# A recurrent block with top-2 experts: logits of all sequences in front, experts' blocks from the ninth FFN tile on

## The reference

```python
xn = layernorm(x)
# branch 1: gated linear recurrence, then a gated FFN
h = rmsnorm(xn) * pre_norm_w
a, i, v = sigmoid(h @ w_a + bias), sigmoid(h @ w_i), h @ w_v
s = sqrt(clip(1 - a*a, 1e-8)) * (i * v)
rec[t] = a[t] * rec[t-1] + s[t]              # scanned in chunks of 64
x1 = xn + rec @ out_proj_w
g, u = split(rmsnorm(x1) * ffn_norm_w @ w_gate_up)   # 2 x 1024 columns
y1 = x1 + (silu(g) * u) @ w_down
# branch 2: top 2 of 8 experts per token
w_tok = softmax over the two largest of xn @ w_router
y2 = sum_e w_tok[e] * (relu(xn @ w_fc[e])**2 @ w_proj[e])
out = x + y1 + y2
```

## Time and profile before

| | us |
|---|---|
| median of 3 runs | 336.8 (336.75 to 338.13) |
| profiled execution | 335.52 |
| its span | 333.8 |
| TensorE busy | 295.5 |
| VectorE busy | 200.8 |
| ScalarE busy | 171.5 |
| POOL busy | 156.3 |

### The profile page before, as it was taken

The page is one execution under the profiler, slowest core; times in us unless marked ns, Lnnn a source line. Parts: engine busy times, 40 slices in busy tenths (PEclk is TensorE's granted clock), DMA queues, the critical chain, the costliest instruction groups (busy, mean ns, idle before and its releaser), DMA issues.

```text
span 333.8 us, 5643 instructions
## 1 busy us (share of the span) xinstructions
PE 295.5 (89%) x1842; PEld 260.8 (78%) x1842; DVE 200.8 (60%) x460; ACT 171.5 (51%) x361; POOL 156.3 (47%) x130
## 2 busy tenths in 40 slices
PE   6589979957685889799899998999999989999993
PEld 6568868746574778698799997889999778888882
DVE  2277747889998984368845555884565552343332
ACT  2669737726836333664336557443655752222220
POOL 5523121500860335748765866786586664316000
PEclk9779979979969899979999999999999999999999
DMA  6999910007030102433433444334443452919931
GB/s 218 355 385 372 422 62 0 0 2 196 0 111 17 34 16 51 65 50 51 66 64 65 65 66 66 64 63 67 67 64 66 64 62 34 165 26 156 226 124 64
DMA packets 31228, 34.29 MB, mean 103 GB/s; under 512 B 5088, under 2 KB 28896, under 8 KB 31168
## 3 DMA queue, kind: packets, MB, share of 16 engines
q0 software_dynamic: 11712, 14.58, 27.7%
q1 hardware_dynamic: 16560, 17.25, 15.2%
q10 hardware_dynamic: 2928, 2.10, 2.0%
HBM read 22.06 MB, written 13.96 MB: 108 GB/s over the span
## 4 chain that ended last, share of the span: by engine, by line
PE 72%; DVE 15%; ACT 4%; issue 3%; DMA 2%; POOL 2%; SPq 1%; DVEq 0%; ACTq 0%; POOLq 0%
PE ps L353 60%; PE ps L411 5%; PE ps L545 4%; DMA X<-in_L_attn_x_dram 2%; PE ps L379 2%; ACT h L704 1%; DVE at_lane L1018 1%; PE ps L424 1%; DVE hT_lo L887 1%; DVE gu L1064 1%; PE ps L362 1%; DVE one_of L1028 1%; DVE dec L921 1%; DVE nblk L984 1%; DVE h2T_lo L936 1%
## 5 line engine op out<-in xcount | busy, mean ns | idle before, releaser
L1281 POOL DMA_INDIRECT xg<-xh_dram,gather_u x39 | 49.5, 1270 | 55.4 <-DVE picks L1094 30.5
L1290 POOL DMA_INDIRECT acc_dram<-yb,gather_u x39 | 62.4, 1599 | 15.2 <-issue 8.6
L353 PE MATMUL ps<-h2T_lo,Wgu_hi 128*128 128x512 f32 x128 | 43.4, 400 | 0.0
L353 PE MATMUL ps<-Wd_hi,guT_hi 128*128 128x256 f32 x128 | 37.2, 291 | 6.8 <-DVE guT_lo L1069 6.8
L353 PE MATMUL ps<-h2T_hi,Wgu_hi 128*128 128x512 f32 x128 | 40.8, 400 | 0.7 <-DVE h2T_lo L936 0.7
L1064 DVE TENSOR_TENSOR gu<-gu,ps 128x512 f32<-128x512 f32 x32 | 21.9, 685 | 30.9 <-PE ps L353 30.8
L353 PE MATMUL ps<-h2T_hi,Wgu_lo 128*128 128x512 f32 x128 | 40.2, 396 | 0.0
L353 PE MATMUL ps<-Wd_hi,guT_lo 128*128 128x256 f32 x128 | 37.0, 289 | 0.0
L353 PE MATMUL ps<-Wd_lo,guT_hi 128*128 128x256 f32 x128 | 37.0, 289 | 0.0
L724 ACT ACTIVATE gu<-ps 128x512 f32<-128x512 f32 x32 | 19.1, 597 | 34.1 <-PE ps L353 34.0
L1111 DVE TENSOR_TENSOR aT_lo<-ps,aT_hi 128x256 fp32r<-128x256 f32 x39 | 16.5, 424 | 27.4 <-ACT aT_hi L754 25.1
(11 more groups left out here) (167 smaller groups left out, 691.6 us busy)
## 6 DMA issues: line engine op xcount, KB each, us to landing
X<-acc_dram POOLq DMA_DIRECT2D x8, 512.0 KB, 9.1
acc_dram<-zero SPq DMA_DIRECT2D x1, 2176.0 KB, 14.3
X<-in_L_attn_x_dram SPq DMA_DIRECT2D x4, 512.0 KB, 8.0
Wgu_raw<-in_L_attn_w_gate_up_dram SPq DMA_DIRECT2D x4, 512.0 KB, 9.8
xh_dram<-X ACTq DMA_DIRECT2D x4, 512.0 KB, 7.5
Wfc_raw<-in_L_ffn_w_fc_dram SPq DMA_DIRECT2D x4, 512.0 KB, 11.5
Wpj_raw<-in_L_ffn_w_proj_dram SPq DMA_DIRECT2D x4, 512.0 KB, 4.0
out_dram<-X SPq DMA_DIRECT2D x3, 512.0 KB, 6.1
```

The costliest lines, as they stand in the source:

```text
L353: return nc.tensor.matmul(dst, lhs, rhs, start=start, stop=stop, skip_group_check=group)
L1281: pool.indirect_dma_start(out=xg[i % XG][:, :], out_offset=None, in_=xh_dram, in_offset=bass.IndirectOffsetOnAxis(ap=gather_u[:, i:i + 1], ...
L1290: pool.indirect_dma_start(out=acc_dram[i % 2], in_=yb[i % YB][:, :], in_offset=None, compute_op=ALU.add, out_offset=bass.IndirectOffsetOnA ...
```

## The change

`FIRST` goes from 4 to 8 and `LAST` from 19 to 24: there are eight bare tiles ahead of the blocks and seven behind them, and 17 tiles with the 39 blocks. Sequence 1's recurrence is run by VectorE among the bare tiles 2 to 4, its output projection by TensorE behind `down(3)` in tile 4, and the transposes of its second norm in tile 6, both in PSUM banks 6 and 7 (`aside`). The projections of sequences 2 and 3 stand behind tiles 11 and 17, the transposes behind 13 and 20, and their recurrences in 9, 10 and 15, 16.

In the front, TensorE has each sequence's transposes and logits earlier among the projections, so that all logits are done before sequence 0's output projection. ScalarE splits a sequence as soon as it is transposed; sequences 2 and 3 are normalised by VectorE instead of ScalarE. VectorE has `take_logits` and `top_two` ahead of sequence 1's gated values, and `take_counts` ahead of sequence 0's residual. The halves of the transposed input get a place each (sequence 3 shares that of 0). The experts' weights are split one by one between the bare tiles. POOL computes the second norm's root for sequence 1 ahead of the first gather.

```diff
+        hT = [(put(f"hT{c}_hi", [P, K, S], F32R, at), put(f"hT{c}_lo", [P, K, S], F32R, at + 4 * KB))
+              for c, at in enumerate((Wpj_hi_at, h2T_at[0], Wpj_hi_at + 8 * KB, Wpj_hi_at))]
         gain = [put(f"gain{b}", [P, K, S], F32, at)
-                for b, at in enumerate((cum_at, Wpj_hi_at, Wpj_hi_at + 4 * KB, cum_at))]
+                for b, at in enumerate((cum_at, cum_at, Wpj_hi_at + 8 * KB, Wpj_hi_at + 12 * KB))]
-        FIRST = 4
-        LAST = 19
-
-        PROJECT = {5: 1, 9: 2, 15: 3}
-        TURN = {6: 1, 12: 2, 18: 3}
+        FIRST = 8
+        LAST = 24
+
+        PROJECT = {11: 2, 17: 3}
+        TURN = {13: 2, 20: 3}
+
+        SLOTS, PROJECT_1, TURN_1 = 3, 4, 6
...
@@ TensorE's queue
-            for n in range(4):
-                aiv(0, n)
+            aiv(0, 0)
+            aiv(0, 1)
             transpose_x(1)
+            aiv(0, 2)
+            aiv(0, 3)
+            logits(0)
             aiv(0, 4)
             aiv(0, 5)
-            logits(0)
+            transpose_x(2)
             aiv(1, 0)
+            logits(1)
             aiv(1, 1)
-            transpose_x(2)
-            for n in range(2, 4):
-                aiv(1, n)
-            logits(1)
-            for n in range(4, 6):
-                aiv(1, n)
             transpose_x(3)
             logits(2)
+            aiv(1, 2)
+            logits(3)
+            aiv(1, 3)
             output_projection(0, 0)
             output_projection(0, 1)
-            logits(3)
-            for n in range(4):
+            aiv(1, 4)
+            aiv(1, 5)
+            count()
+            for n in range(6):
                 aiv(2, n)
-            count()
             transpose_h2(0, 0)
             transpose_h2(0, 1)
-            aiv(2, 4)
-            aiv(2, 5)
             for n in range(6):
                 aiv(3, n)
             for d in range(FIRST):
                 gate_up(d, 0)
                 gate_up(d, 1)
-                if d == 2:
+                if d == SLOTS:
                     slots()
                 if d:
                     down(d - 1)
+                if d == PROJECT_1:
+                    output_projection(1, 0)
+                    output_projection(1, 1)
+                if d == TURN_1:
+                    transpose_h2(1, 0)
+                    transpose_h2(1, 1)
...
@@ ScalarE's queue
             store_xh(0)
-            normalise_x(1)
             split_h(0)
             copy_xh(0)
+            normalise_x(1)
             store_xh(1)
             decay(0, 0)
             decay(0, 1)
-            normalise_x(2)
+            split_h(1)
+            copy_xh(1)
             input_gate(0, 0)
             input_gate(0, 1)
-            split_h(1)
+            store_xh(2)
             decay_squares(0)
+            split_h(2)
             gains(0)
-            copy_xh(1)
-            store_xh(2)
-            normalise_x(3)
+            copy_xh(2)
+            store_xh(3)
+            split_h(3)
+            copy_xh(3)
...
@@ VectorE
+            def normalise_x(c):
+                dve.wait_ge(rstd_ready, c + 1)
+                for j in range(J):
+                    t = J * c + j
+                    last = V.tensor_scalar(X[c][:, j, :], X[c][:, j, :], mv[:, t, 0:1], rn1[:, t:t + 1],
+                                           ALU.subtract, ALU.mult)
+                last.then_inc(xh_ready[c], 1)
...
             statistics(3)
+            normalise_x(2)
             split_h(1)
+            normalise_x(3)
+            scales()
             gated_value(0, 0)
             gated_value(0, 1)
-            scales()
+            split_h(2)
             signal(0, 0)
             signal(0, 1)
             cumulate(0, 0)
             recur(0, 0)
-            split_h(2)
+            split_h(3)
             cumulate(0, 1)
             recur(0, 1)
-            split_h(3)
+            take_logits()
+            top_two()
             gated_value(1, 0)
             gated_value(1, 1)
+            take_counts()
             add_residual(0, 0)
             add_residual(0, 1)
-            take_logits()
-            top_two()
-            take_counts()
             place_tokens()
...
             lanes(1)
+            split_gu(0)
             lanes(2)
-            split_gu(0)
-            lanes(3)
             gate(1)
             up(1)
-            experts()
+            lanes(3)
             split_gu(1)
-            block_list()
-            weights_lo(9)
-            up(2)
-            weights_lo(10)
-            split_gu(2)
             signal(1, 0)
             signal(1, 1)
+            up(2)
+            experts()
+            split_gu(2)
+            cumulate(1, 0)
+            recur(1, 0)
+            up(3)
+            block_list()
+            split_gu(3)
+            cumulate(1, 1)
+            recur(1, 1)
+            up(4)
             signal(2, 0)
+            split_gu(4)
+            add_residual(1, 0)
+            add_residual(1, 1)
...
@@ POOL's queue
             for n in range(6, 9):
                 weights_lo(n)
+            root_h2(1)
             pool.wait_ge(routed, 1)
```

More of the change, by code:

```diff
@@ L204, in recurrent_moe_block @@
         dve_chain, pool_chain = sem("dve_chain"), sem("pool_chain")
-        var_ready, rstd_ready, xh_ready = sem("var_ready"), sem("rstd_ready"), sem("xh_ready")
+        var_ready, rstd_ready = sem("var_ready"), sem("rstd_ready")
+        xh_ready = [sem(f"xh_ready{b}") for b in range(B)]
         xh_stored = [sem(f"xh_stored{b}") for b in range(B)]
@@ L395, in aiv @@
                     for k in range(K):
-                        last = product(ps[:, rec_bank(b, n), :], Waiv[l][:, k, col:col + P], hT[b % 2][h][:, k, :],
+                        last = product(ps[:, rec_bank(b, n), :], Waiv[l][:, k, col:col + P], hT[b][h][:, k, :],
                                        m + k == 0, m == 2 and k == K - 1)
@@ L410, in output_projection @@
                     for k in range(K):
-                        last = nc.tensor.matmul(ps[:, side, (j % 2) * D:(j % 2 + 1) * D],
+                        last = nc.tensor.matmul(ps[:, aside(b) + side, (j % 2) * D:(j % 2 + 1) * D],
                                                 dec[b][:, k, j * P:(j + 1) * P], Wo[:, k, :], start=k == 0, stop=k == K - 1)
@@ L423, in transpose_h2 @@
                 for j in range(J):
-                    last = nc.tensor.transpose(ps[:, k, j * P:(j + 1) * P], h2[b][:, j, k * P:(k + 1) * P], ident[:, :])
+                    last = nc.tensor.transpose(ps[:, aside(b) + k, j * P:(j + 1) * P], h2[b][:, j, k * P:(k + 1) * P], ident[:, :])
                 last.then_inc(h2T_done, 1)
@@ L648, in normalise_x @@
                                         bias=nb1[:, t:t + 1])
-                last.then_inc(xh_ready, 1)
+                last.then_inc(xh_ready[c], 1)
             def store_xh(c):
-                act.wait_ge(xh_ready, c + 1)
+                act.wait_ge(xh_ready[c], 1)
                 act.dma_start(xh_t[c], X[c][:, :, :]).then_inc(xh_stored[c], 16)
@@ L817, in _ @@
             gate(1)
-            for b in range(1, B):
-                gains(b)
+            gains(1)
+            gains(2)
+            gains(3)
             split_gu(1)
@@ L822, in _ @@
             weights_hi(9)
-            weights_hi(10)
             split_gu(2)
             gate(3)
+            weights_hi(10)
+            split_gu(3)
+            gate(4)
             weights_hi(11)
+            split_gu(4)
+            squares(1)
+            gate(5)
             weights_hi(12)
-            split_gu(3)
-            for n in range(13, 16):
-                weights_hi(n)
+            split_gu(5)
+            normalise(1)
+            gate(6)
+            weights_hi(13)
+            split_gu(6)
+            split_h2(1)
+            gate(7)
+            weights_hi(14)
+            split_gu(7)
+            weights_hi(15)
             weights_hi(ALL - 1)
@@ L886, in split_h @@
                     dve.wait_ge(hT_hi, K * c + k + 1)
-                    V.scalar_tensor_tensor(out=hT[c % 2][1][:, k, :], in0=ps[:, TX + k, :], scalar=pre_w[:, k:k + 1],
-                                           in1=hT[c % 2][0][:, k, :].bitcast(F32), op0=ALU.mult,
+                    V.scalar_tensor_tensor(out=hT[c][1][:, k, :], in0=ps[:, TX + k, :], scalar=pre_w[:, k:k + 1],
+                                           in1=hT[c][0][:, k, :].bitcast(F32), op0=ALU.mult,
                                            op1=ALU.subtract).then_inc(hT_split, 1)
@@ L935, in split_h2 @@
                     dve.wait_ge(h2T_hi, K * b + k + 1)
-                    V.scalar_tensor_tensor(out=h2T[b % 2][1][:, k, :], in0=ps[:, k, :], scalar=ffn_w[:, k:k + 1],
+                    V.scalar_tensor_tensor(out=h2T[b % 2][1][:, k, :], in0=ps[:, aside(b) + k, :], scalar=ffn_w[:, k:k + 1],
                                            in1=h2T[b % 2][0][:, k, :].bitcast(F32), op0=ALU.mult,
```

86 lines of the change are left out of this document (43 added, 43 removed).

## The result

The changed kernel takes 320.02 us (median of 4 runs, 319.29 to 320.68) against 336.97 us of the kernel before in the same comparison: a ratio of 0.949, 95% interval 0.9458 to 0.9522. Predicted were 319.0 us. The profiled execution took 319.69 us, with a span of 317.9.

The account below looks back on a forecast made before the run. TensorE, busy 89% of the span, was taken as the bound. Gains 10.4 - 3.3 + 11.7 - 1.0 = 17.8 us bring the span from 333.8 to 316.0, the profiled execution to 317.7, the median to 319.0; range 310 to 331.

Parts of the forecast that it names:

- the four stages: Front gain 10.4 us, bare tiles -3.3, blocks 11.7, tail -1.0.
- The term of 2.77: Front: splitting sequence 0 before normalising sequence 1 removes TensorE's 2.77 us idle ahead of the first projection.
- the 15.40: Front: time in us at which TensorE is free and the first projection should start, instead of 18.17.
- The idle for logits(3): Front: new TensorE idle of 1.8 us, as ScalarE's copy stands behind VectorE's first recurrence half.
- the walk: Step-by-step pass through four engine queues in the diff's order; put tile 0's start at 64.7 us.
- 10.4: Front: gain in us at tile 0, after taking off half of the half clock's 1.9.
- the 0.25 taken: Front: price in us of each of eight normalising instructions moved to VectorE, between 0.21 and 0.34.
- Behind it the pattern of 144.01 to 275.24 stays: Blocks behind tile 8: 131.2 us for 122.9 of work, so 8.3 us lost as before.
- (a): Bare tiles: VectorE's handoffs cost more, 53.9 us instead of 49.1, first block 2 later; 326 us in all; chance 0.17.
- (b): Front: no clock falls and the 1.8 idle vanishes, 314 us; chance 0.70 shared with the forecast.
- (c): Front hangs on something other than ScalarE's order, say loads of x; first 11 us stay away: 330 to 336; chance 0.08.
- (d): Tail: accumulating loads run one behind another's landing, eight take 73 us; median 363; chance 0.05.

Follow-up runs that it names:

- the first experiment: Kernel before with only ScalarE's split and copy of sequence 0 moved ahead of normalising sequence 1: 329.76 us, ratio 0.9833.
- front and blocks together: Kernel before with the changed front alone: ratio 0.9625; changed kernel with the old front's orders: 0.9783; both changes together: 0.949.
- the blocks alone: Changed kernel with the front's orders of the kernel before; FIRST 8, LAST 24 and sequence 1 between bare tiles stay: 328.5 us, ratio 0.9783.
- the gathers first: Changed kernel with root_h2(1) behind POOL's first four gathers instead of ahead: 319.07 us, ratio 0.9513.
- six splits on VectorE: Changed kernel with POOL's splits of weight pieces 3 to 8 done by VectorE: 317.57 us, ratio 0.9448.
- three splits on VectorE: Changed kernel with POOL's splits of weight pieces 6 to 8 done by VectorE: 318.1 us, ratio 0.9494.
- six of them and `take_down(2)` late: Changed kernel with POOL's splits of pieces 3 to 8 on VectorE and take_down(2) behind the last block's aT_lo: 317.84 us, ratio 0.9455.
- the fastest: Changed kernel with six splits on VectorE, take_down(2) late, sequence 1's output projection in tile 5, up(3), up(4) before recurrence halves: 315.67 us, ratio 0.9421.

## Why the prediction was right, and where only by luck

The method, losses of each stage against TensorE's work at full clock, gave 319.0 for 320.02, and the four stages moved the way it said. That the two times lie 1.0 apart is in part luck: the gain forecast from the profile was 17.8 us, two profiles of the changed kernel gave 15.9 and 14.6, and the medians 17.0, as the profile of the kernel before was a quick one.

- **Front.** The term of 2.77 is shown by the first experiment, where the start moved by 3.4; the first projection started at 15.74 in the changed kernel, 0.3 behind the 15.40. The idle for logits(3), which the walk put at 1.8, is 1.42. The half clock behind it was counted as half. It is missing in the first profile and there in full in the second, and so the 10.3 that matches 10.4 was the better draw, and the other 7.5. In the seven profiles with this front, tile 0 started between 65.50 and 69.06, never as early as the 64.7 of the walk. `place_tokens` ended at 59.1 for 58.5.
- **Normalising on VectorE.** Four steps took 1.38 us, 0.35 each, the upper of the two bounds and not the 0.25 taken. One alone took 0.41 for 256 columns, where the 0.42 of the earlier trace rows is for 512. So a subtract and multiply by two values per partition does not run at that rate; the Trainium skill's tier table (VectorE: DVE Perf Modes) has it at twice, and here the measurement differs. It was hidden, as said.
- **Bare tiles.** 49.0 us for 49.1, and 47.3 in the second profile, where the half clock that the sum priced at 1.5 stayed away from the output projection. The waits stood where the walk had them: 0.63, 2.14, 3.16, none and 1.67 in the second profile, for 1.2, 1.6, 3.7, 1.3 and 2.3. The prices of VectorE's steps were wrong in the parts. The prediction took the long steps of the trace of before as the price of those steps (6.6 us for `experts`). They are the price of POOL's splits, which move with POOL's queue. `experts` got short, two signals took 5.66 instead of 1.3. The same six splits of POOL were in both kernels, and so the sum held: that is luck. That it would not have held if the change had moved POOL's work to another place is an argument; the nearest run is the one with two more POOL steps, where the stretch grew by 3.1.
- **Blocks.** 10.1 for 11.7. The step that failed is "Behind it the pattern of 144.01 to 275.24 stays": `take_down(2)` now falls into the last tile of blocks, which has a third block and the leftover steps. TensorE's wait there was 1.05 in the kernel before and is 1.85; put late, `take_down(2)` gives the 0.8 back. Another 0.8 was lost in tile 8: 9.16 us from 114.64 to 123.80, where the walk had 8.4 (a tile and two blocks, 7.94, less the 1.6 in the pipeline, plus 2.1). Its waits were 1.20 and 1.16 for 0.7 and 1.2.
- **Tail.** 1.3 for 1.0, by the measured stream of 2.7 us a load; half of the loads taken away give 2.1 back. By the estimate from the Trainium skill's fixed 2.0 us for each load (DMA: Bandwidth & Descriptors, Anatomy of one DMA) the tail would have cost about 4. The loads overlap, and the stream is the better price.
- **Rivals.** Of (a), that VectorE's handoffs eat more, the profile has nothing; (b), a front without the idle and with no fall of the clock, did not come: the idle of 1.42 is there, and the clock falls; (c) is out, since the front moved when ScalarE's order alone did; (d) is out, as the loads do run beside one another, though the median to landing grew from 9.1 to 11.3.

What stays open: why front and blocks together give about 2 us less than their ratios multiplied. The intervals just touch, and the half clock of one output projection (1.7 us) is enough to make it. Open too is what decides where the clock falls in the front.

## What to carry to other kernels

Price a change of order by the loss of each stage against the bound engine's work, then walk the queues; here the sum of gains, 17.8, stood against 14.6 to 17.0 measured. Take a second profile before a stage that matches is called right: the front's gain was 10.3 in one and 7.5 in the other. Before a duration is carried to another place, compare it with its neighbours of the same shape: a step of 40 columns that takes 1.7 us is waiting for something, and here it was the other engine's long SBUF step. An engine that seems off the path (POOL) can be on it through the one it blocks: two useless POOL steps cost 2 to 3 us.

## What the runs showed of the hardware

Where TensorE's clock falls to its half (1.2 GHz) differed between executions of one kernel, and with it the price of a wait. The output projection of sequence 1 shows it in eleven profiles of kernels with nearly the same orders around it:

| profiles | clock ahead of it | wait in front of it | it took |
|---|---|---|---|
| the changed kernel, the one with half of the loads, the one with `take_down(2)` late | at half once, behind the wait of 2.1 for `down(1)` | 1.89, 1.90, 1.90 | 5.41 each time |
| the changed kernel again, the blocks alone, the gathers first | at half once, behind the wait of 3.1 to 3.2 for `down(2)` | 1.67, 1.69, 1.75 | 3.72 each time |
| six splits on VectorE, two more POOL steps | at half behind waits of 2.24 and 6.21, and back | 0.65, 1.13 | 3.72 |
| three splits on VectorE, six of them and `take_down(2)` late | at half behind a wait of 2.2, and still so | 1.50, 1.07 | 5.85, 5.57 |
| the fastest | did not fall | 0.16 | 3.72 |

In the first profile of the changed kernel the granted clock was 0.51 from 79.5 to 82.9 and 0.50 from 97 to 100, within the projection; in the second it was 0.50 from 90.8 to 94.0 and 1.00 in the projection. So the length of the last wait alone does not tell: 1.50 and 1.07 stand in front of slow projections whose clock had fallen before them. A wait of 1.9 came with 1.7 us more, and where the clock falls anew varies; that this makes a good part of the spread of 2 to 5 us between runs of one kernel is likely, but not shown, as most kernels have one profile.
